# Decoder layer on one core: the offset of the attention codes by one product per pair, and late weight integers on ScalarE

## The reference, cut to what matters

```
qkv  = fq_floor(fq_floor(h) @ fq_round(w_qkv))
dots = fq_floor(einsum("bhnd,bhmd->bhnm", q, k) * temp)
attn = fq_floor(softmax(dots))          # scale is a power of two, codes clip(floor(attn / s), -128, 127)
out  = einsum("bhnm,bhmd->bhnd", attn, v)
out  = fq_floor(fq_floor(out) @ fq_round(w_out))
```

## Time and profile before

| | |
|---|---|
| Runs, us | 464.04, 465.09, 488.02 |
| Median of the runs | 465.09 |
| Profiled execution: own time / span | 465.23 / 463.5 |
| Mean granted TensorE clock | 0.686 |
| Instructions | 6753 |
| VectorE / ScalarE / TensorE busy | 406.4 / 345.9 / 241.0 us |

### The profile page before, as it was taken

One profiled execution on the slowest core, in us unless ns is written; L12 is line 12 of the kernel. 1 busy time (PEld: TensorE's weight loads), 2 busy tenths in 40 slices (PEclk: granted clock), 3 DMA queues, 4 the chain that ended last, 5 costly groups with the idle time before them and its releaser, 6 DMA issues.

```text
span 463.5 us, 6753 instructions
## 1 busy us (share of the span) xinstructions
PE 241.0 (52%) x1541; PEld 103.7 (22%) x1541; DVE 406.4 (88%) x1293; ACT 345.9 (75%) x789; POOL 144.3 (31%) x321
## 2 busy tenths in 40 slices
PE   1488987876777723333322333069994827015031
PEld 0464423331222110000000000023341815012031
DVE  5868998888799999999999999687977986977967
ACT  2599966798999928999999999926776565428033
POOL 2400000001000003999999999940000006420010
PEclk9889988999555555555555555559998867557556
DMA  7600000000544430999999998790004000000002
GB/s 270 156 0 2 0 1 1 23 23 25 188 174 182 158 128 32 204 191 211 188 204 198 206 199 179 133 199 0 1 1 150 5 0 1 1 0 0 0 0 93
DMA packets 84247, 43.21 MB, mean 93 GB/s; under 512 B 69095, under 2 KB 74487, under 8 KB 84090
## 3 DMA queue, kind: packets, MB, share of 16 engines
q1 hardware_dynamic: 82650, 42.69, 36.0%
q10 hardware_dynamic: 1568, 0.21, 0.3%
HBM read 7.75 MB, written 1.58 MB: 20 GB/s over the span
## 4 chain that ended last, share of the span: by engine, by line
DVE 35%; ACT 27%; PE 20%; issue 15%; ACTq 1%; DMA 1%; DVEq 0%; SPq 0%
ACT mem L950 20%; PE ps L471 19%; DVE mem L1072 6%; DVE mem L1232 4%; DVE d_max L1075 4%; DVE mem L1495 3%; DVE m L1632 2%; DVE m L1633 2%; ACT mem L884 2%; ACT mem L920 2%; ACTq L950 1%; DVE mem L1283 1%; DVE mem L1502 1%; DMA mem<-in_x 1%; DVE c L1071 1%
## 5 line engine op out<-in xcount | busy, mean ns | idle before, releaser
L471 PE MATMUL ps<-mem 64*128 64x256 bf16 (+5 forms) x1188 | 182.2, 357 | 113.0 <-DVE row_max L1324 80.0
L950 ACT ACTIVATE mem<-mem,neg_max 128x256 f32<-128x256 int16 x256 | 125.8, 492 | 9.2 <-DVE neg_max L1071 9.2
L471 PEld LDWEIGHTS ps<-mem 64*128 64x128 bf16 (+3 forms) x1188 | 68.0, 120 | 219.2 <-DVE row_max L1324 108.6
L1324 DVE CUSTOM_DVE_ANT_0 mem<-ps,fold,c 128x256 int16<-128x256 f32 x256 | 110.9, 471 | 0.2 <-DVE fold L1072 0.2
L429 POOL TENSOR_SCALAR mem<-mem,r_now 128x256 int16<-128x256 f32 x176 | 81.0, 480 | 77.1 <-DVE r_now L1071 77.0
L1232 DVE TENSOR_TENSOR mem<-mem 128x1024 bf16<-128x1024 bf16 x76 | 49.8, 686 | 5.6 <-ACT mem L884 3.7
L900 ACT ACTIVATE mem<-ps,c 128x1024 bf16<-128x1024 f32 x48 | 48.3, 1296 | 1.8 <-PE ps L471 1.8
L950 ACT ACTIVATION_READ_ACCUMULATOR mem<-mem,neg_max x256 | 47.6, 186 | 0.0
L920 ACT ACTIVATE mem<-ps,c 128x1024 int16<-128x1024 f32 x32 | 36.2, 1209 | 10.3 <-DVEq L1267 6.4
L1075 DVE TENSOR_REDUCE d_max<-ps 128x1 f32<-128x1024 f32 (+1 forms) x34 | 37.9, 1125 | 3.6 <-PE ps L471 3.5
L429 POOL TENSOR_SCALAR bv_fine<-mem,r_now 128x256 int16<-128x256 f32 x80 | 36.6, 477 | 2.6 <-DVE r_now L1071 2.5
(11 more groups left out here) (203 smaller groups left out, 363.3 us busy)
## 6 DMA issues: line engine op xcount, KB each, us to landing
mem<-mem SPq DMA_DIRECT2D x64, 256.0 KB, 2.3
mem<-in_L_attn_w_qkv SPq DMA_DIRECT2D x1, 1536.0 KB, 8.5
mem<-in_x SPq DMA_DIRECT2D x4, 256.0 KB, 4.2
mem<-in_x SPq DMA_DIRECT2D x1, 1024.0 KB, 5.5
out<-mem SPq DMA_DIRECT2D x4, 256.0 KB, 2.2
xattn_matrix<-mem SPq DMA_DIRECT2D x1, 512.0 KB
mem<-in_L_attn_w_out SPq DMA_DIRECT2D x1, 512.0 KB, 4.7
mem<-in_L_ffn_W SPq DMA_DIRECT2D x2, 256.0 KB, 5.0
```

The lines of the kernel that those rows point to most:

```text
L471: return te.matmul(o_, l_, r_, start=start, stop=stop)
L950: ins = sc.activation(e_ring[:, u % 4, pos], y_ring[:, u % 4, pos], ACT.Exp, scale=scale_reg, bias=neg_max[:, u % 4, pos:pos + 1], accum_o ...
L1324: ins = ve.tensor_tensor_reduce(y_ring[:, slot, pos], ps[:, 2 * slot + pos // 2, (pos % 2) * N:(pos % 2 + 1) * N], shift, col("g_dots"), - ...
```

## The change

The offset leaves each pair by one product in place of two. Because `minus` is constant, v times `minus` is -129 times the sum of v over all 256 keys of the batch, the same for every query. These sums are formed once: PE adds v_codes over the keys with 32 products (8 batches x 2 halves of the heads x 2 `mc`), each with a slice of `pick` as 64 columns of weights, in which only the columns `row` and `row + 32` are one. So row `row` and row `row + 32` of bank 1 (64 partitions x 512) both hold the sum of v for one batch and one half of the heads. ACT copies all 64 rows to bf16 (`v_sums`), and DVE replaces the upper 32 by what that rounding lost (the float32 sum less its bf16 part), so that the two rows together are exact. The pair's product then has 64 rows of `v_sums` as weights, and as its other operand one column of the new `minus` (64 x 16, with -129 at `row` and `row + 32`), repeated 256 times by the access pattern. The 32 products stand between the last scores and `across(0, diag, 1)` on PE, ACT's copy behind the last exponential, DVE's subtraction between sending the diagonal and taking the result.

The integers of w_out, W1 and W2 move from DVE to ACT, behind step 7 of its evictions; DVE's casts to bf16 move to groups 21, 22 and 23, PE's transposes from group 23 to 27, ACT's evictions of w1T and w2T from step 12 to 14. The memset of `minus` on POOL goes; the memsets and selects of `pick` and `minus` are put behind the temperature. `bk_sel` and `v_sums` share a tile. The semaphores `cs_r2_ps` and `cs_r2` are renamed, since they count a second use.

```diff
@@ gpsimd
-            pl.memset(minus[:], -OFFSET)
...
+            link(pl.memset(pick[:], 0.0))
+            pl.memset(pick[:, 15:16], 1.0)
+            pl.memset(pick[:, 47:48], 1.0)
+            link(pl.memset(minus[:], 0.0))
+            link(pl.affine_select(out=minus[:], in_=minus[:], compare_op=ALU.not_equal, fill=-OFFSET,
+                                  base=0, pattern=[[-1, 2 * B]], channel_multiplier=1))
+            pl.affine_select(out=minus[:], in_=minus[:], compare_op=ALU.not_equal, fill=-OFFSET,
+                             base=-32, pattern=[[-1, 2 * B]], channel_multiplier=1).then_inc(sem("ctx_ones"), 1)
@@ tensor, behind the last unit of scores
+            pe.wait_ge(sem("cast_v"), GROUPS * len(QKV_CODE_DVE))
+            pe.wait_ge(sem("cast_a"), GROUPS * (QKV_UNITS - len(QKV_CODE_DVE)) + 4)
+            pe.wait_ge(sem("ctx_ones"), 2)
+            pe.wait_ge(sem("y_ready_u"), B * DOT_UNITS + 1)
+            for row in range(2 * B):
+                b, half = row // 2, row % 2
+                for mc in range(2):
+                    last = mm(ps[0:64, 1, :], pick[:, 15 - row:79 - row],
+                              v_codes[:, 2 * b + mc, half * BANK:(half + 1) * BANK],
+                              row == 0 and mc == 0, row == 2 * B - 1 and mc == 1)
+            last.then_inc(sem("sums_ps"), 1)
             across(0, diag, 1)
             pe.wait_ge(sem("attn_scale"), 1)
-
-
-            pe.wait_ge(sem("cast_v"), GROUPS * len(QKV_CODE_DVE))
-            pe.wait_ge(sem("cast_a"), GROUPS * (QKV_UNITS - len(QKV_CODE_DVE)) + 4)
+            pe.wait_ge(sem("v_sums"), 1)
@@ tensor, each pair
-                    for mc in range(2):
-                        mm(ps[:, bank, cols], v_codes[:, 2 * b + mc, pair * P:(pair + 1) * P], minus[:],
-                           mc == 0, False)
+                    row = 2 * b + pair // 4
+                    mm(ps[:, bank, cols], v_sums[:, (pair % 4) * P:(pair % 4 + 1) * P],
+                       minus[:, row:row + 1].to_broadcast((64, N)), True, False)
@@
-                if grp == 23:
+                if grp == 27:
                     pe.wait_ge(sem("mlp_codes"), 1)
@@ scalar, behind the exponentials
+            act.wait_ge(sem("sums_ps"), 2)
+            sc.activation(v_sums, ps[0:64, 1, :], ACT.Copy).then_inc(sem("sums_kept"), 1)
+
+            def late_integers():
+                act.wait_ge(sem("late_max"), 4)
+                for last in range(B * GROUPS - FINE_RING, B * GROUPS):
+                    act.wait_ge(sem(f"transposed{last % FINE_RING}"), 16 + 16 * (last // FINE_RING))
+                sc.activation(w_out_i.rearrange("p j d -> p (j d)"), w_out_f.rearrange("p j d -> p (j d)"), ACT.Copy,
+                              scale=i4[:, 3:4]).then_inc(sem("w_out_i"), 1)
+                sc.activation(w1_i.rearrange("p j d -> p (j d)"), w1_f.rearrange("p j d -> p (j d)"), ACT.Copy,
+                              scale=i2w[:, 0:1]).then_inc(sem("mlp_i"), 1)
+                sc.activation(w2_i, w2_f, ACT.Copy, scale=i2w[:, 1:2]).then_inc(sem("mlp_i"), 1)
...
-                if nth == 12:
+                if nth == 7:
+                    late_integers()
+                if nth == 14:
                     act.wait_ge(sem("mlp_T_ps"), 1)
@@ vector
-            across(col("m"), 1, diag, 0, col("x"), 1)
+            across_send(col("m"), 1, diag, 1)
+            dve.wait_ge(sem("sums_kept"), 2)
+            ve.tensor_tensor(v_sums[32:64], ps[32:64, 1, :], v_sums[32:64], ALU.subtract).then_inc(sem("v_sums"), 1)
+            across_take(1, 0, col("x"))
@@ vector, late_weights
                 if grp == 13:
-                    for last in range(B * GROUPS - FINE_RING, B * GROUPS):
-                        dve.wait_ge(sem(f"transposed{last % FINE_RING}"), 16 + 16 * (last // FINE_RING))
                     link(ts(s2w[:], x6[:, 4:6], 1.0 / 127, TINY, ALU.mult, ALU.max))
-                    ts(w_out_i, w_out_f, i4[:, 3:4], None, ALU.mult).then_inc(sem("w_out_i"), 1)
-                    link(ve.reciprocal(i2w[:], s2w[:]))
-                if grp == 15:
+                    ve.reciprocal(i2w[:], s2w[:]).then_inc(sem("late_max"), 1)
+                if grp == 21:
                     dve.wait_ge(sem("w_out_i"), 1)
                     ve.tensor_copy(w_out_codes, w_out_i).then_inc(sem("w_out_codes"), 1)
-                    ts(w1_i, w1_f, i2w[:, 0:1], None, ALU.mult).then_inc(sem("mlp_i"), 1)
-                if grp == 17:
-                    ts(w2_i, w2_f, i2w[:, 1:2], None, ALU.mult).then_inc(sem("mlp_i"), 1)
-                    dve.wait_ge(sem("mlp_i"), 1)
+                if grp == 22:
+                    dve.wait_ge(sem("mlp_i"), 2)
                     ve.tensor_copy(w1_n, w1_i)
-                if grp == 19:
-                    dve.wait_ge(sem("mlp_i"), 2)
+                if grp == 23:
                     ve.tensor_copy(w2_n, w2_i).then_inc(sem("mlp_codes"), 1)
```

More of the change, by code:

```diff
@@ L183, in decoder_layer @@
         ident_b = sb("ident_b", [P, P], BF16)
-        minus = sb("minus", [P, N], BF16)
+        pick = sb("pick", [P, 79], BF16)
+        minus = sb("minus", [64, 2 * B], BF16)
         ones_b = sb("ones_b", [3, P], BF16)
@@ L195, in decoder_layer @@
                      bv_fine[:].bitcast(I16).rearrange("p (u n) -> p u n", n=UNIT)]
-        bk_sel = sb("bk_sel", [B, B, D])
+        bk_wide = sb("bk_wide", [P, B * D])
+        bk_sel = bk_wide[0:B].rearrange("p (b d) -> p b d", d=D)
+        v_sums = bk_wide[0:64].bitcast(BF16)[:, 0:BANK]
         bkv = sb("bkv", [B, 2, D])
@@ L527, in sums_of_ctx @@
                 mm(ps[0:B, 7, D:2 * D], cs_col, xw_T[:, 1], True, False)
-                mm(ps[0:B, 7, D:2 * D], s512[:], bkv[0:1, 1], False, True).then_inc(sem("cs_r2_ps"), 1)
+                mm(ps[0:B, 7, D:2 * D], s512[:], bkv[0:1, 1], False, True).then_inc(sem("sums_ps"), 1)
             def a1_main(half, b):
@@ L551, in ctx_work @@
                 if n == 36:
-                    pe.wait_ge(sem("cs_r2"), 1)
+                    pe.wait_ge(sem("sums_kept"), 1)
                     a1_bias(0)
@@ L865, in ctx_evictions @@
                 if n == 30:
-                    act.wait_ge(sem("cs_r2_ps"), 1)
+                    act.wait_ge(sem("sums_ps"), 1)
                     sc.activation(cs_r2[:].rearrange("p k d -> p (k d)"), ps[0:B, 7, 0:2 * D], ACT.Copy)\
-                        .then_inc(sem("cs_r2"), 1)
+                        .then_inc(sem("sums_kept"), 1)
                 if n == 45:
```

## The result

The changed kernel took 478.62 us (median of 4 runs, 477.67 to 478.79) against 466.21 for the kernel before (4 runs: 464.04, 465.09, 467.34 and 488.02). The ratio is 1.028, with a 95% interval from 1.023 to 1.033. The forecast was 457.8, in a range from 455.3 to 461.6: wrong in direction, and outside the range. The profiled execution took 477.67 with a span of 475.9, which is 12.4 us more than before.

What follows compares the result with a forecast made beforehand. TensorE was taken to bound the attention-times-v stage. Its saving of 7.5 us less 0.1 for moved work gave -7.4, so 465.1 became 457.7, stated as 457.8 us; the 8-in-10 range was 455.3 to 461.6.

Steps and rivals of the forecast that it cites:

- 5.7 us at the slow clock: Start of the attention-times-v stage: 1.2 GHz for 5.7 us as before, holding 6.2 pairs after the change, then 2.4 GHz.
- 0.538: TensorE time in us for one pair of heads at 2.4 GHz after the change, against 0.663 before.
- 1.2 was booked: TensorE in the stage: weight transposes and the maximum across partitions add about 1.2 us before the last absolute-value eviction.
- the first rival: Clock already high at the stage's start because of the sums; VectorE then limits; -9.6 us, 455.5; chance 0.10.
- The fourth: Rival: passage between product shapes costs more than the product saved; at 0.10 more each, +4.8 us, 470; chance 0.06.
- The chance of 0.03 for slower: Whole kernel: chance given to being slower by over 2%, 474.4 us or more; within 2% got 0.81.
- The removed product: One offset product fewer per pair on TensorE saves its short interval: 0.12 us, or 0.19 at the slow clock.
- Half of the two, 0.16: Rival: the offset product saves its full half, 0.16 us, pair 0.50; total near 456; chance 0.08.
- The repeated column: The offset product's moving operand, one column repeated 256 times: costed at nothing, up to 0.1 as the other end.
- The sums: 32 products in TensorE's idle time ahead of the stage, from 290.1 to 299.9; cost nothing.
- The moved conversions: Integers moved to ScalarE behind step 7: VectorE stands 1.2 us; cost 0 to 0.3, taken as 0.1 us.
- VectorE and ScalarE keep up: In the stage: VectorE has 9.7 us to spare against 7.5 wanted; ScalarE needs 1.84 against TensorE's 2.15 per two groups.

Runs made afterwards that it cites:

- e1: Changed kernel with 128 rows in the offset product, the added 64 rows of both operands zero; 462.97 us, ratio 0.994 to the kernel before.
- e3: Kernel before with its two offset products cut to 64 rows each, four passes a pair, no sums; 492.76 us, one execution.
- e4: Kernel before with the second of its two 128-row offset products left out, three passes a pair, no sums; 463.43 us, one execution.
- f1: e1 plus unread dense products ahead of the stage: 16 behind the sums of v, 8 behind the reduction across partitions; 457.77 us, ratio 0.983.
- f2: Changed kernel, 64-row offset product kept, plus the same 16 and 8 unread dense products as f1; 458.58 us, one execution.
- e2: Changed kernel, 64 rows, with a stored tile of 256 columns of -129 in place of the one repeated column; 478.82 us, one execution.
- f4: f1 with the three integer conversions of the late weights back on VectorE; 457.81 us, ratio 0.984.
- g1: e1 with the float32 product of the late maxima moved from behind group 6 to behind group 10, no added products; 477.42 us, one execution.
- h1: Same kernel as f1, timed over five more executions; 457.29 to 457.88 us, ratio 0.983.
- g4: e1 with only the 8 unread dense products behind the reduction across partitions; executions 458.60, 457.06, 457.08 and 457.58 us.
- h3: Changed kernel with 8 unread dense products right behind the float32 product of group 6, none ahead of the stage; 466.27 us, one execution.
- g3: Changed kernel, 64 rows, with only the 8 unread dense products behind the reduction across partitions; executions 457.48, 458.48, 457.47 and 479.09 us.

## Why the prediction was wrong

**The step that failed** is the one that took "5.7 us at the slow clock" from the stage before and put it into the stage after, as if the clock rose with time. It was treated as a property of the stage's length, and it depends on the products in it. 53.8 of the 60 pairs were priced at 0.538 and ran at 0.893: 53.8 x 0.355 = 19.1 us, of the 20.3 between the forecast's start of the last absolute-value eviction and the measured one (342.3 and 362.55). The rest is nearly all the transposes and the float32 product, 2.6 us at the slow clock where 1.2 was booked. The cause is the rows of the offset product: with 128 of them the changed kernel gets its clock back (e1), and with 64 of them the kernel before did not get it (e3). The pass removed has its own part: even with 128 rows the rise came after 15 to 16.6 us (e1, e4) and not after 5.7, and the time was 463.

f1 (457.77) is the forecast's change with the clock given back, and lands on its 457.8. That is partly luck. In f1 the slow stretch is gone too, which is worth 2.4 us (6.2 pairs take 3.3 us and not 5.7). Against it stand smaller terms: the pair is 0.559 on average and not 0.538 (23.47 us for the 42 pairs from 315.70 to the transposes, so 1.3 us in 60), the stage begins 0.3 us later, TensorE waits some 0.3 us for VectorE, and the transposes with the float32 product take 0.1 more than booked. From 313.86 to the eviction at 341.95 the chain of f1 lies on TensorE, so VectorE is not what held it there, as the first rival at 455.5 had supposed.

**The rivals.** None had the mechanism. The first looked at the clock in one direction only, whether it would be up at the start. It was not: it fell at 304.3, 5.0 us after the sums. The fourth was on the right side with the wrong reason: the passage cost no more than before (0.21 us from the start of the 64-row product to the next at the full clock in f2, 320.55 - 320.34, against 0.20). The chance of 0.03 for slower was drawn from prices of instructions and had no place for the clock.

**Point by point.**
- The removed product is worth its short interval. The forecast had pairs of 0.92 and 0.54 us; they are 0.89 (changed kernel) and 0.55 (f2). Half of the two, 0.16, would have made 0.50. The Trainium skill (TensorEngine Tiling (Array Packing), section Key Properties) says that a change of the tiling mode drains the engine. The trace agrees in kind: both passages stay.
- The repeated column costs nothing at the slow clock: e2 without it takes the same time. At the full clock no run takes it away; the 0.21 us above leaves room for 0.01.
- The sums: 8.87 us from 290.43, over at 299.3, with the clock rising at 294.1, against a forecast end of 299.9; hidden, as were copy and subtraction.
- The moved conversions: forecast a stand of VectorE of 1.2 us behind ScalarE, ahead of the conversion of group 22; 1.28 in f1, at that place. The forecast booked 0.1 us of cost for the move and counted on the VectorE time that it frees; f4, without the move, takes the same time.
- VectorE and ScalarE keep up at the full clock: in f1 TensorE is busy 34.73 of 35.20 us, though VectorE is busy 33.50 of them.
- The clock high from the start needed dense work up to the stage (f1, f2), and then it was high. The sums alone ended 7 us ahead of the stage.

The Trainium skill (TensorE: Matmul & The Clock Gate, section What's actually happening) says that the throttled state is the default and activity releases it. The trace agrees in kind, but being busy without a gap did not release it here: TensorE was busy 50.50 of 50.50 us at 0.50.

## What to carry to other kernels

Before taking products away from a stage on TensorE, or rows out of them, ask what lifted its clock there: a stage that is busy without a gap can still sit at 1.2 GHz (e3, with half the rows in its offset products; g1, with one 128-row product fewer in a pair), and a saving of 0.11 us a pair was answered by 0.34. Padding the offset product's rows with zeros costs no time for a product (a pair is 0.55 us either way) and gave the short time in all 17 executions, together with dense products in the idle time ahead of the stage. That version (h1, 457.55 us) is 1.7% below the kernel before and 4.4% below the changed one. Eight such products right ahead of the stage did as well (g4, 457.33). And a clock's rise read from the old profile belongs to the old mix of products; a profile of the new one is needed before a time at the full clock is promised.

## What the runs showed of the hardware that was not expected

- Rows count for the clock and not for the time. With 64 or 128 rows the offset product takes the same 0.89 us pair at 1.2 GHz and the same 0.55 at 2.4 (changed kernel and e1, f2 and f1), but with two 64-row products in a pair of four passes the clock was at 0.50 for 68 us (e3, one execution), where with 128 rows it had risen after 5.7.
- Lifting and holding differ. Pairs of three passes with 128 rows ran for 54 us before it rose (g1) and held it for 35 us once it was up (f1). With 64 rows they never came up by themselves (changed kernel, e2) and held it for 35.8 us in f2, but 6 of 15 executions with added products were long.
- What stood just before each rise: 3.6 us of the sums of v, the eight added products (h3, g3, g4), the transposes at the end of g1, the float32 product of 1.6 us in e1, whose 10 times all lie near 463. All of it is products with 128 rows and no 64-row product among them. It need not fill the array's columns: the sums use 64 columns of weights. That one of these is the cause of its rise is shown for the added products only (h3, one execution, against the changed kernel, where nothing else differs).
- Open: why the float32 product behind group 10 (g1) did not do what it does behind group 6 (a pause of 1.02 us follows it there), why the 64-row form holds in one execution and not in the next, and how much of the late rise belongs to the rows and how much to the passes.
